# A graph layer's edge loop on one core: the weighting of each block as four VectorE instructions, one per place in the rows

## What is computed

```python
h = (x @ W.T).reshape(n, H, D)                       # H = 8 heads, D = 32
alpha = einsum('ehd,hd->eh', h[src], a_src) + einsum('ehd,hd->eh', h[dst], a_dst)
alpha = alpha + sum(relu(edge_attr @ edge_W.T + edge_b).reshape(-1, H, D) * h[dst], axis=-1)
alpha = where(alpha >= 0, alpha, 0.2 * alpha)
ex = exp(alpha - segment_max(alpha, dst)[dst])
attn = ex / maximum(segment_sum(ex, dst)[dst], 1e-10)
out = segment_sum(h[src] * attn[..., None], dst)     # divided by the sum at the end
return out.reshape(n, H * D) + bias
```

## Time and profile before

| | |
|---|---|
| median of 3 runs | 3437.85 us (3424.1 to 3450.0) |
| the profiled execution | 3451.68 us, of it span 3449.9 us |
| PE busy | 2388.1 us, 69% |
| DVE (VectorE) busy | 2338.7 us, 68%, 3523 instructions |
| POOL (GpSimd) busy | 2100.4 us, 61% |
| ACT (ScalarE) busy | 948.9 us, 28% |
| granted TensorE clock, mean | 0.802 of full |

### The profile page before, as it was taken

One profiled execution on the slowest core, in us unless ns is written; L12 is line 12 of the kernel. 1 busy time (PEld: TensorE's weight loads), 2 busy tenths in 40 slices (PEclk: granted clock), 3 DMA queues, 4 the chain that ended last, 5 costly groups with the idle time before them and its releaser, 6 DMA issues. The chain is left out here.

```text
span 3449.9 us, 45436 instructions
## 1 busy us (share of the span) xinstructions
PE 2388.1 (69%) x8886; PEld 1577.9 (46%) x8886; DVE 2338.7 (68%) x3523; ACT 948.9 (28%) x3079; POOL 2100.4 (61%) x2041
## 2 busy tenths in 40 slices
PE   1600177877877777778777787777777554349998
PEld 1400045545544554444445454445454332128887
DVE  6689677777777777777777777777777555452223
ACT  3500032222222222222222222222222121143332
POOL 2320377777777777777777777777777552526000
PEclk9855588888888888888888878888888777559999
DMA  8210255555555555555555555555556994210000
GB/s 264 80 65 26 69 155 160 161 159 160 160 157 156 157 158 157 152 157 158 154 155 156 158 157 154 157 157 156 155 156 150 114 120 67 74 45 6 18 18 32
DMA packets 322416, 437.60 MB, mean 127 GB/s; under 512 B 115526, under 2 KB 257832, under 8 KB 322132
## 3 DMA queue, kind: packets, MB, share of 16 engines
q0 software_dynamic: 90000, 262.14, 31.2%
q1 hardware_dynamic: 231540, 174.91, 17.6%
q10 hardware_dynamic: 848, 0.26, 0.0%
HBM read 351.33 MB, written 85.74 MB: 127 GB/s over the span
## 5 line engine op out<-in xcount | busy, mean ns | idle before, releaser
L856 POOL DMA_INDIRECT src_in<-t_node_rows,rec_in x1760 | 1882.9, 1070 | 611.7 <-issue 532.2
L904 PE MATMUL p_sum<-weighted,hot 128*128 128x264 f32 x3520 | 1130.1, 476 | 226.5 <-DVE weighted L1088 225.8
L904 PEld LDWEIGHTS p_sum<-weighted,hot 128*128 128x128 f32 x3520 | 799.1, 234 | 521.3 <-issue 191.1
L1043 DVE SCALAR_TENSOR_TENSOR prod<-p_enc,near 128x512 f32<-128x512 f32 x880 | 561.6, 678 | 286.2 <-ACT near L967 282.7
L1047 DVE TENSOR_REDUCE dots<-prod 128x32 f32<-128x1024 f32 x440 | 536.8, 1220 | 15.2
L1088 DVE TENSOR_TENSOR weighted<-src_in,weighted 128x1024 f32<-128x1024 f32 x440 | 535.2, 1217 | 10.2 <-ACT weighted L973 9.2
L871 PE MATMUL p_pick<-ident,hot 128*128 128x128 f32 x440 | 156.5, 356 | 381.6 <-ACT hot L951 381.4
L951 ACT ACTIVATE hot<-apart 128x128 f32<-128x128 f32 x440 | 136.1, 309 | 971.4 <-PE p_sum L904 971.0
L885 PE MATMUL p_pick<-win,hotT 128*128 128x272 f32 x880 | 362.8, 498 | 43.9 <-DMA win<-t_node_rows 43.6
L967 ACT COPY near<-p_pick 128x272 f32<-128x272 f32 x440 | 169.9, 386 | 567.7 <-PE p_pick L885 567.7
L880 PE MATMUL p_enc<-expander,attrT 30*128 30x256 bf16 x1760 | 305.7, 298 | 3.3 <-DMA attrT<-t_block_attr 3.3
(11 more groups left out here) (293 smaller groups left out, 1767.7 us busy)
## 6 DMA issues: line engine op xcount, KB each, us to landing
win<-t_node_rows SPq DMA_DIRECT2D x440, 136.0 KB, 2.6
t_block_sums<-sums SPq DMA_DIRECT2D x110, 528.0 KB, 3.5
src_in<-t_node_rows,rec_in POOLq DMA_INDIRECT x1760, 2.8
attrT<-t_block_attr SPq DMA_DIRECT2D x330, 36.0 KB
flags_in<-t_block_flags SPq DMA_DIRECT2D x440, 4.0 KB
t_node_rows<-out_rows SPq DMA_DIRECT2D x49, 136.0 KB, 1.7
x<-in_x SPq DMA_DIRECT2D x4, 1536.0 KB, 26.1
out_x<-x SPq DMA_DIRECT2D x48, 128.0 KB
```

The costliest lines, as they stand in the source:

```text
L856: pool.indirect_dma_start(src[:, q.par, b, k, :], None, scr["rows"], bass.IndirectOffsetOnAxis(ap=rec_i[:, q.par, b, k:k + 1], axis=0)).th ...
L904: last = nc.tensor.matmul(p_sum[b % 2][:, 0:ROW], hot[:, q.par, b, :], weighted[:, b, k, :], start=(k == 0), stop=(k == W - 1))
L1043: nc.vector.scalar_tensor_tensor(prod[:, b % 2, 2 * half:2 * half + 2, :], p_enc[(PAIRS * b + half) % len(p_enc)][:, :, :], 0.0, near[:, q ...
```

## The change

`weigh` issues four instructions where it issued one. Each covers one of the four places (128 x 256 values) in place of all (128 x 4 x 256). Only the last of the four counts the semaphore up, so TensorE and GpSimd are told at the same point as before: when the whole block is weighted. Sources, destination, values and the order of everything else are unchanged.

```diff
             def weigh(q, b):
                 if b == 0:
                     dve.wait_ge(s["weight"], q.s + 1)
-                heads = lambda v: v.rearrange("p k (h d) -> p k h d", h=H)
-                nc.vector.tensor_tensor(heads(weighted[:, b, :, 0:D]), heads(src[:, q.par, b, :, 0:D]),
-                                        spread(weighted[:, b, :, D:ROW], HD), ALU.mult).then_inc(s["weighted"], 1)
+                for k in range(W):
+                    last = nc.vector.tensor_tensor(weighted[:, b, k, 0:D].rearrange("p (h d) -> p h d", h=H), src[:, q.par, b, k, 0:D].rearrange("p (h d) -> p h d", h=H),
+                                                   spread(weighted[:, b, k, D:ROW], HD), ALU.mult)
+                last.then_inc(s["weighted"], 1)
```

## The result

The kernel with four weighting instructions takes 3292.3 us (median of 4 runs, 3288.6 to 3296.1). The kernel before took 3432.0 us beside it. The ratio is 0.959, with a 95% interval of 0.954 to 0.963. It is 4.1% faster, inside the range of 3275 to 3390 and 32 us better than the forecast of 3324. The two profiled spans differ by more, 3449.9 - 3294.3 = 155.6 us, since the profiled execution of before (3451.7 us) lay above all four of its runs (3424.1 to 3450.0).

A forecast was written before the change was run, and what follows sets the result against it. The prediction took GpSimd's rate of gathers as the bound. Steady part -127, given back +10, last steps +2.4, four last groups +1 make -114 us, from 3437.85 to 3324 us; range 3275 to 3390.

The forecast's parts named there:

- What paces the loop: Edge loop: GpSimd's gathers run without a pause, 1.074 us each plus 0.305 between, 16 making a step of 22.05 us.
- What makes a gather long: GpSimd: a running `weigh` holds a gather to its end, raising the mean to 1.074 us from a median of 0.946.
- the rival built on it: Edge loop: `weigh` doesn't hold gathers, they stay at 1.07 us and the time at 3438 us; chance 0.08.
- VectorE's own price: VectorE: four instructions at a pair's 0.34 us pitch add 0.22 us a block, +0.9 a step; full durations, +1.9.
- How long a gather waits in a group: GpSimd: a gather arriving among the four instructions waits 0.18 us; groups cover 27.7%, so 0.049 us a gather, saving 127.
- 0.13 us point: GpSimd: 0.13 us after its start a gather needs something that a running `weigh` holds; its last 0.82 us follow.
- The check of 232 against 218 us: Gathers before the change: random arrivals in `weigh` would cost 232 us; the gathers' excess over the median length was 218.
- The factor 0.94: Gathers: agreement of the 218 us excess with the 232 us worked out, applied to the waits expected with four instructions.
- The others keep up: VectorE needs 20.4 us of the 20.8 us step, TensorE 17.3; 10 us given back for steps where this fails.
- VectorE as the bound: Edge loop: VectorE takes over at 21.3 to 21.7 us a step, 3363 to 3408 us; chance 0.16.
- Slower by a hold through the group: GpSimd: a gather arriving in a group waits for all of it, 0.72 us on the mean, +100 us, 3538; chance 0.07.
- Better than forecast: Gathers: most fall outside the groups, another 30 to 50 us go, 3275 to 3295; counted in the forecast's 0.69.

The follow-up runs named there:

- all six kernels of the undisturbed profiles: The kernel before (3432.0 us), and its weighting in four instructions (3292.3), two (3323.1), eight (3292.0), or replaced by one reduction (3257.8) or four (3263.1).
- the run with one reduction: Against the kernel with four instructions: weighting left out, one reduction of the same source values (one SBUF input) in its place; 3257.8 us, ratio 0.943 to the kernel before.

## Why the prediction was right, step by step

**What paces the loop.** Right. GpSimd fills the stretch before and after, and in all six kernels of the undisturbed profiles the distance from one gather to the next stays at 0.305 to 0.307 us on the mean, so the step (20.07 to 22.06 us) moves with the gathers' length alone.

**What makes a gather long.** Right, and shown by taking the second SBUF input away (1.070 to 0.949 us with VectorE's time unchanged), and by the 816 gathers that L1043 and L1047 left alone. The Trainium skill (SBUF — State Buffer, "Who interferes with whom") has the lock for two SBUF inputs, and all runs agree with it. Its inference that a tensor_tensor leaves descriptor generation alone doesn't carry over to these gathers: the rival built on it, no change at 3438 us, fell. Whether it is descriptor generation that is held, or the gather's reading of its row numbers from `rec_in`, no run here tells apart.

**VectorE's own price.** The bound chosen, the pair's pitch, held: starts 0.335 us apart (0.34 taken), groups 1.42 us wide (1.44), +0.2 us a block. The upper bound of full durations is excluded.

**How long a gather waits in a group.** This term was mis-sized, and it is most of the distance to the forecast. It was put at 0.18 us on the mean over 27.7% of the time, 0.049 a gather; measured in steps 5 to 100 it is 0.971 - 0.946 = 0.025. Over the 1611 gathers of the sum that is 39 us, of the 42 by which the profiled spans' 155.6 exceed the forecast's 114. In the trace of after 527 gathers reach their 0.13 us point inside a group, 30% of them all, so the share was right. But 135 of these lost nothing, and the 392 that were held lost 0.10 us each, so that all 527 lost 0.076 us on the mean and not 0.18. Sorting the gathers by their start shows the fault. A gather that starts up to about 0.03 us after the start of an instruction is not held by it, and one that starts in its last 0.13 us isn't either. So of each instruction some 0.16 us do not count: of 1.22 us that is little, of 0.42 it is more than a third. With n instructions of d us a block, and gathers that start at random, the time lost per gather is then about n (d - 0.16)^2 / 2 over a block's 5.1 to 5.5 us. The 0.16 was read off these same traces, so the table checks how the loss falls with d and not the 0.16 itself. The measured column also holds about 0.003 us that other VectorE instructions cost (the run with one reduction: 0.949 against 0.946).

| instructions a block | d | worked out | measured, steps 5 to 100 | step |
|---|---|---|---|---|
| 1 | 1.217 | 0.101 | 0.128 | 22.06 |
| 2 | 0.685 | 0.053 | 0.047 | 20.78 |
| 4 | 0.420 | 0.026 | 0.025 | 20.44 |
| 8 | 0.284 | 0.012 | 0.027 | 20.47 |

The last row is above its value by the gathers that were kept through several instructions. The first is above it because the gathers don't arrive at random: 356 were held where some 337 would be at random, and they lost 0.60 us on the mean where half of 1.06 would be 0.53. The check of 232 against 218 us had hidden this, since it assumed random arrivals and the full 1.217 us, and the two faults nearly cancelled for one long instruction. The factor 0.94 drawn from it had no meaning for short ones.

**The others keep up.** Right, and better than feared: the 10 us given back did not occur. GpSimd has no wait over 0.3 us for `weighted` in 450 to 2450, and only the three waits of 1.1 us beside. VectorE's wait at L1055 went from 255.9 us in 2220 to 97.3 in 2000, about 2.5 to 1.0 us a step; 0.5 was forecast.

**The sum.** Forecast: -127 in the steady part, +10 given back, +2.4 in the last steps, +1 at the end. Measured between the profiles: L1055 of step 101 starts at 2489.1 in place of 2650.7, -161.6. That of the last step starts at 2723.0 in place of 2881.8, -158.8, so the last steps gave back 2.8. The span's end is at -155.6, another 3.2. So the steady part is 35 us better than its term and nothing to speak of was given back there. The runs of both kernels on one chip give -140 (3432.0 to 3292.3), since the profiled execution of before was a long one. That is 26 of the 32 us between forecast and median; the other 6 are the median of before, which came out at 3432.0 with a fourth run where the forecast started from 3437.85.

**The rivals.** VectorE as the bound: not with four, and not quite with eight. Slower by a hold through the group: it doesn't happen at 0.42 us, but does now and then at 0.28. Better than forecast, counted in with it at 3275 to 3295: its time is what came, but not for its reason. It had most gathers fall outside the groups, and 30% reached their point inside one, slightly more than the 27.7% of random arrivals; they lost less because 0.16 us of each instruction do not count. That the time landed in this band is luck. A case that I did not have, a loop that gathers do not pace at all, is the one in which the change ended slower.

## What to carry to other kernels

When GpSimd issues gathers back to back and its mean is above its median, look at which VectorE instruction ends a fixed time before each long one; if it reads two SBUF operands, cut it into pieces of some 0.4 us. Here that cost VectorE 0.2 us a block and brought the loss per gather from 0.128 to 0.025 us: a held gather loses at most the rest of one instruction, and the 0.16 us that don't count are a larger part of a short one. Pieces near 0.28 us brought nothing more that the runs could tell. Before trusting such a gain, see what paces the loop on the chips it will run on: a faster queue is worth nothing where the loop waits for another.

## What the hardware showed that I had not expected

A gather is held only if it starts between 0.03 us after the start and 0.13 us before the end of a VectorE instruction with two SBUF inputs (L1088, L1061), and it then ends 0.82 us after that instruction's end. With such instructions 0.20 us apart some gathers are passed over for up to 0.7 us, as at 1571.80, though the same does not happen at 0.335 us. And SyncE's twelve loads of a step, 8.6 us on two chips, took 16 to 18 us in two later groups of runs, with single instructions of 0.56 us and more; in the same groups the unchanged kernel before took 15 and 20% longer (3946 and 4118 us against 3432).
